# Two-layer attention and mixture-of-experts kernel: the second layer's chunked attention in a pipelined order, with transpositions and a second PSUM bank

## What is computed

```python
# attention of layer 1, 16 heads of 16, chunks of 128 tokens, S is the carried state of a head
scores  = einsum('bchd,bshd->bhcs', qb, kb) * D          # D: causal mask with a decay of each head
o_intra = einsum('bhcs,bshd->bchd', scores, vb)
o_inter = einsum('bchd,bhde->bche', qb, S) * q_decay
S_new   = chunk_decay * S + einsum('bshd,bshe->bhde', kb * k_decay, vb)
o = o_intra + o_inter                                     # then times sigmoid(gate)
o = o * rsqrt(mean(o*o over a head) + EPS) * norm_w       # group norm
attn = o @ Wo
# experts of layer 1: 8 experts, two for each token
y_e = (silu(x @ w_gate[e]) * (x @ w_up[e])) @ w_down[e]   # weighted and summed over the two experts
x = x + attn + moe
```

## Time and profile before

| | |
|---|---|
| median of 3 runs | 1006.86 us (1006.46 to 1008.85) |
| the profiled execution, its time | 1003.08 us |
| its span, first to last instruction | 1001.3 us |
| mean granted clock of PE, as a share of 2.4 GHz | 0.913 |
| busy: PE, DVE, ACT, POOL | 846.0, 574.8, 394.3, 312.0 us |

### The profile page before, as it was taken

One profiled execution on the slowest core, in us unless ns is written; L12 is line 12 of the kernel. 1 busy time (PEld: TensorE's weight loads), 2 busy tenths in 40 slices (PEclk: granted clock), 3 DMA queues, 4 the chain that ended last, 5 costly groups with the idle time before them and its releaser, 6 DMA issues. The chain is left out here.

```text
span 1001.3 us, 14864 instructions
## 1 busy us (share of the span) xinstructions
PE 846.0 (84%) x4544; PEld 486.2 (49%) x4544; DVE 574.8 (57%) x1269; ACT 394.3 (39%) x676; POOL 312.0 (31%) x250
## 2 busy tenths in 40 slices
PE   4989999858988997998988767399999899999963
PEld 3765655501223443433433546166666565666642
DVE  7746877268878776778673428234434333443437
ACT  2336666424664565466547413022222222222210
POOL 2034566363001331051015203233333443333231
PEclk9999999956998998999999966599999999999985
DMA  8524655462321332433403303899953444333243
GB/s 266 140 60 146 200 188 185 138 193 80 96 70 52 113 101 94 157 105 116 137 22 117 116 21 117 219 271 355 176 128 93 97 109 119 90 91 85 75 134 133
DMA packets 158354, 130.26 MB, mean 130 GB/s; under 512 B 64129, under 2 KB 139921, under 8 KB 158289
## 3 DMA queue, kind: packets, MB, share of 16 engines
q1 hardware_dynamic: 151136, 109.89, 38.0%
q0 software_dynamic: 7152, 19.54, 6.6%
HBM read 83.37 MB, written 46.01 MB: 129 GB/s over the span
## 5 line engine op out<-in xcount | busy, mean ns | idle before, releaser
L1305 DVE TENSOR_REDUCE b_negmax<-b_psM 128x1 f32<-128x512 f32 x256 | 163.0, 682 | 59.1 <-PE b_psM L1491 56.2
L1242 ACT ACTIVATE b_probs<-b_psE 128x512 f32<-128x512 f32 x256 | 138.8, 595 | 125.7 <-PE b_psE L1509 124.6
L1491 PE MATMUL b_psM<-b_kst,b_qst 96*128 96x512 bf16 x256 | 99.7, 432 | 38.5 <-DVE b_negmax L1305 22.5
L1509 PE MATMUL b_psE<-b_qst,b_kst 98*128 98x512 bf16 x256 | 88.1, 406 | 14.3 <-ACT b_probs L1242 9.6
L1863 POOL DMA_INDIRECT scratch_ys<-d_y,put x39 | 40.2, 1030 | 150.7 <-ACT d_y L1895 149.5
L2019 PE MATMUL d_psG<-d_w,d_xT 128*128 x156 | 76.6, 614 | 3.6 <-issue 1.7
L1518 PE MATMUL b_psV<-b_probs,b_vst 128*32 128x512 f32 x512 | 73.8, 650 | 3.1 <-ACT b_probs L1242 3.1
L2044 PE MATMUL d_psY<-d_w,d_hidden 128*128 x312 | 75.2, 384 | 0.0
L2027 PE MATMUL d_psU<-d_w,d_xT 128*128 x156 | 75.1, 604 | 0.0
L1491 PEld LDWEIGHTS b_psM<-b_kst,b_qst 96*128 96x128 bf16 x256 | 24.5, 99 | 98.4 <-DVE b_negmax L1305 73.5
L1509 PEld LDWEIGHTS b_psE<-b_qst,b_kst 98*128 98x128 bf16 x256 | 20.4, 99 | 103.2 <-issue 53.6
(11 more groups left out here) (353 smaller groups left out, 1593.6 us busy)
## 6 DMA issues: line engine op xcount, KB each, us to landing
scratch_parts<-a_parts SPq DMA_DIRECT2D x12, 512.0 KB, 4.3
b_qst<-scratch_parts SPq DMA_DIRECT2D x96, 64.0 KB, 2.1
b_kst<-scratch_parts SPq DMA_DIRECT2D x96, 64.0 KB, 2.1
scratch_parts<-b_part SPq DMA_DIRECT2D x24, 256.0 KB, 3.6
d_qst<-scratch_parts SPq DMA_DIRECT2D x96, 64.0 KB, 2.7
d_kst<-scratch_parts SPq DMA_DIRECT2D x96, 64.0 KB, 3.0
scratch_ys<-a_y SPq DMA_DIRECT2D x39, 128.0 KB, 1.8
scratch_v<-a_xn SPq DMA_DIRECT2D x4, 1024.0 KB, 6.9
```

The source lines that it names most:

```text
L1242: nc.scalar.activation(probs[k % PSLOTS][:, h, :], psE[h % 2][:, :], ACT.Exp, scale=float(HD) ** -0.5).then_inc(scores_used[h % 2], 1)
L1305: nc.vector.tensor_reduce(negmax[i][:, t, h:h + 1], psM[:, h % 2, :], AX_X, ALU.max, negate=True).then_inc(rows_used[h % 2], 1)
L1491: nc.tensor.matmul(psM[:, h % 2, :], qst[g][0:STACK, h, t * P:(t + 1) * P], kst[g][0:STACK, h, :], start=True, stop=True).then_inc(rows_re ...
L1509: nc.tensor.matmul(psE[h % 2][:, :], kst[g][0:STACKM, h, k * P:(k + 1) * P], qst[g][0:STACKM, h, :], start=True, stop=True).then_inc(score ...
```

## The change

- `main_order`: a chunk's steps are now `own` n, `outputs` n, `scores` 0 to 2 of chunk n+1, `normalise` n, `scores` 3 of chunk n+1, `turn_normed` n, `project` n. Nine steps a chunk instead of twelve, 148 in all instead of 192, with no empty ones, and all of them are dealt out over the expert rounds. Behind the last `down` come only `turn_normed` 15, `project` 15 and the four `combine`.
- `outputs` on PE turns `headsT` by four transpositions into ps0 in place of eight selection matmuls. The rows of a head then lie 32 columns apart (`spread`). The carried state's product goes into a bank of its own (psT, the first half of a new bank ps2).
- `gate_out` on DVE: for chunks with c > 0 it copies psT to `o`, adds `spread` to it, and then multiplies by `sg`, each behind the one before: three instructions ahead of `gated` instead of one. It now stands in the same step as `outputs`, as does POOL's power.
- Banks: `turn_normed` writes psT, `project` writes the other half of ps2 (psO).
- Waits: `scores` 0 of chunk n+1 waits for `gated` of chunk n instead of `o_done`; `scores` 1 for `update_done`; `outputs` and `project` for `o_done`; `turn_normed` for `normT_done`.
- SP no longer loads `sel` (32 KB). Its other loads, their order and their waits stay.

```diff
@@ main_order
-    steps = [(n, s) for n in range(CHUNKS) for s in range(LSTEPS)]
-    tail = LSTEPS + LSTEPS // 2
+    steps = [("scores", 0, g) for g in range(GROUPS)]
+    for n in range(CHUNKS):
+        ahead = [("scores", n + 1, g) if n + 1 < CHUNKS else ("rest", n, g) for g in range(GROUPS)]
+        steps += [("own", n, 0), ("outputs", n, 0), *ahead[0:3], ("normalise", n, 0), ahead[3],
+                  ("turn_normed", n, 0), ("project", n, 0)]
...
-            while given < (len(steps) - tail) * used // slots:
-                order.append(("light", *steps[given]))
+            while given < len(steps) * used // slots:
+                order.append(steps[given])
                 given += 1
-    combine = {4: 0, 6: 1, NORMALISE: 2, PROJECT: 3}
...
+    return order + [("combine", b, 0) for b in range(BATCHES)]
@@ layer1_main
-        ps0, ps1 = (ps(f"ps{i}", [P, SEQ]) for i in range(2))
+        ps0, ps1, ps2 = (ps(f"ps{i}", [P, SEQ]) for i in range(3))
+        spread = ps0[:, :].rearrange("p (h w) -> p h w", w=VW)
+        psT, psO = ps2[:, 0:KT * P], ps2[:, KT * P:KT * P + D]
@@ gate_out (DVE)
-                nc.vector.tensor_tensor(o[:, :], ps0[:, 0:D], sg[s][:, :], ALU.mult).then_inc(gated[s], 1)
+                mixed = o[:, :].rearrange("p (h d) -> p h d", d=HD)
+                if c:
+                    nc.vector.tensor_copy(o[:, :], psT).then_inc(carried, 1)
+                    dve.wait_ge(carried, 2 * (n - n // NC) - 1)
+                    nc.vector.tensor_tensor(mixed, spread[:, :, 0:HD], mixed, ALU.add).then_inc(carried, 1)
+                    dve.wait_ge(carried, 2 * (n - n // NC))
+                nc.vector.tensor_tensor(mixed, mixed if c else spread[:, :, 0:HD],
+                                        sg[s][:, :].rearrange("p (h d) -> p h d", d=HD), ALU.mult).then_inc(gated[s], 1)
@@ scores (PE)
-                    pe.wait_ge(o_done, n)
+                    if n:
+                        pe.wait_ge(gated[(n - 1) % CSLOTS], (n - 1) // CSLOTS + 1)
                 elif g == 1:
-                    pe.wait_ge(normT_done, n)
+                    pe.wait_ge(update_done, updates_before(n))
@@ outputs (PE)
+                updates(n)
...
+                pe.wait_ge(o_done, n)
+                for g in range(GROUPS):
+                    mm = nc.tensor.transpose(ps0[:, g * CH:(g + 1) * CH], headsT[:, g * CH:(g + 1) * CH], ident[:, :])
                 if c:
                     for k in range(KT):
-                        nc.tensor.matmul(ps0[:, k * P:(k + 1) * P], qd[n % CSLOTS][:, k * P:(k + 1) * P], state[:, k, :],
-                                         start=k == 0, stop=False, skip_group_check=True)
-                for g in range(GROUPS):
-                    mm = nc.tensor.matmul(ps0[:, g * HG * HD:(g + 1) * HG * HD], headsT[:, g * CH:(g + 1) * CH], sel[:, :],
-                                          start=c == 0 and g == 0, stop=g == GROUPS - 1, skip_group_check=True)
+                        mm = nc.tensor.matmul(psT[:, k * P:(k + 1) * P], qd[n % CSLOTS][:, k * P:(k + 1) * P],
+                                              state[:, k, :], start=True, stop=True, skip_group_check=True)
@@ turn_normed, project (PE)
-                    mm = nc.tensor.transpose(ps1[:, k * P:(k + 1) * P], normed[:, k * P:(k + 1) * P], ident[:, :])
+                    mm = nc.tensor.transpose(psT[:, k * P:(k + 1) * P], normed[:, k * P:(k + 1) * P], ident[:, :])
...
-                    mm = nc.tensor.matmul(ps0[:, 0:D], normT[:, k, :], wo[:, k, :], start=k == 0, stop=k == KT - 1)
+                    mm = nc.tensor.matmul(psO, normT[:, k, :], wo[:, k, :], start=k == 0, stop=k == KT - 1, skip_group_check=True)
```

More of the change, by code:

```diff
@@ L1673 @@
 UPDATES = NC - 1
-LSTEPS = 12
 CSLOTS = 3
-NORMALISE, TURN, PROJECT = LSTEPS - 3, LSTEPS - 2, LSTEPS - 1
 WCOLS = KT * H1 * 2 + HT1 * D
 def main_order():
-    steps = [(n, s) for n in range(CHUNKS) for s in range(LSTEPS)]
-    tail = LSTEPS + LSTEPS // 2
+    steps = [("scores", 0, g) for g in range(GROUPS)]
[3 more added lines that the diff above has]
+                  ("turn_normed", n, 0), ("project", n, 0)]
     order = [("turn", 0, 0), ("turn", 1, 0), ("gate", 0, 0), ("up", 0, 0), ("turn", 2, 0)]
@@ L1731, in layer1_main @@
         y = [sb(f"y{i}", [P, D]) for i in range(YSLOTS)]
-        ident, sel, blockmask = sb("ident", [P, P]), sb("sel", [P, HG * HD]), sb("blockmask", [P, P])
+        ident, blockmask = sb("ident", [P, P]), sb("blockmask", [P, P])
         normw, neghalf, wo = sb("normw", [P, D]), sb("neghalf", [P, HEADS]), sb("wo", [P, KT, D])
@@ L1755, in layer1_main @@
         heads_copied, update_ps, update_done, state_done = (sem(n) for n in ("heads_copied", "update_ps", "update", "state"))
+        carried = sem("carried")
         out_ps, squared, summed, ss_done, rs_done = (sem(n) for n in ("out_ps", "squared", "summed", "ss", "rs"))
@@ L1759, in layer1_main @@
         back_in, half_added, added, stored = sems("back_in", BATCHES), sem("half_added"), sem("added"), sem("stored")
-        CONSTS = 16 * 4
+        CONSTS = 16 * 3
         CHUNK_IN = 16 * (2 * len(Q_PARTS) + 4)
@@ L1818, in _ @@
             load_weights(1)
-            for dst, src in ((sel[:, :], io["sel16"]), (blockmask[:, :], io["blockmask"]),
+            for dst, src in ((blockmask[:, :], io["blockmask"]),
                              (normw[:, :], io["norm_w"].to_broadcast((P, D))),
@@ L1864, in down, with outputs @@
                                              y[b % YSLOTS][:, :], None).then_inc(put_out[b % YSLOTS], 16)
[L1866 to L1869, removed]
+            def outputs(n, _):
+                pool.wait_ge(ss_done, n + 1)
+                nc.gpsimd.tensor_tensor(rs[:, :], ss[:, :], neghalf[:, :], ALU.pow).then_inc(rs_done, 1)
             for b in range(XSLOTS):
@@ L1874, in _ @@
             pool.wait_ge(neghalf_set, 1)
-            walk({"light": light, "turn": turn, "down": down})
+            walk({"outputs": outputs, "turn": turn, "down": down})
         @block.scalar
@@ L1895, in down, with own, turn_normed @@
                 nc.scalar.activation(y[b % YSLOTS][:, :], psY[:, 0:D], ACT.Copy).then_inc(y_done, 1)
[L1897 to L1908, removed]
+            def own(n, _):
+                act.wait_ge(probs_used, n + 1)
+                act.wait_ge(out_ps, n)
+                nc.scalar.activation(headsT[:, :], ps0[:, :], ACT.Copy).then_inc(heads_copied, 1)
+            def turn_normed(n, _):
+                act.wait_ge(normT_ps, n + 1)
+                act.wait_ge(o_ps, n)
+                nc.scalar.activation(normT[:, :, :], psT.rearrange("p (k n) -> p k n", k=KT), ACT.Copy).then_inc(normT_done, 1)
+            walk({"own": own, "turn_normed": turn_normed, "gate": gate, "turn_h": turn_h, "down": down})
         @block.vector
@@ L1954, in gate_out, with normalise @@
                 nc.vector.tensor_scalar(ss[:, :], ss[:, :], 1.0 / HD, EPS, ALU.mult, ALU.add).then_inc(ss_done, 1)
-            def normalise(n):
+            def normalise(n, _):
                 dve.wait_ge(rs_done, n + 1)
@@ L1962, in normalise, with residual, outputs @@
                 nc.vector.tensor_tensor(normed[:, :], o[:, :], normw[:, :], ALU.mult).then_inc(normed_done, 1)
-            def residual(n):
+            def residual(n, _):
                 dve.wait_ge(o_ps, n + 1)
[L1966 to L1978, removed]
+                nc.vector.tensor_tensor(xacc[:, n, :], psO, xacc[:, n, :], ALU.add).then_inc(o_done, 1)
+            def outputs(n, _):
+                take_update(n)
+                gate_out(n)
             def combine(b, _):
@@ L1990, in combine @@
                     last.then_inc(added if i else half_added, 1)
-            walk({"light": light, "turn": turn, "up": up, "combine": combine})
+            walk({"scores": weigh, "outputs": outputs, "normalise": normalise, "project": residual, "turn": turn, "up": up,
+                  "combine": combine})
         @block.tensor
@@ L2060, in scores, with own @@
                 mm.then_inc(scores_ps[g], 1)
-            def own(n):
+            def own(n, _):
                 for g in range(GROUPS):
@@ L2079, in updates, with outputs @@
                 mm.then_inc(update_ps, 1)
-            def outputs(n):
+            def outputs(n, _):
                 c = n % NC
+                updates(n)
                 pe.wait_ge(consts_in, CONSTS)
@@ L2096, in outputs, with turn_normed @@
                 mm.then_inc(out_ps, 1)
-            def turn_normed(n):
+            def turn_normed(n, _):
                 pe.wait_ge(normed_done, n + 1)
-                if n % NC < NC - 1:
-                    pe.wait_ge(update_done, updates_before(n) + 1)
+                pe.wait_ge(normT_done, n)
                 for k in range(KT):
-                    mm = nc.tensor.transpose(ps1[:, k * P:(k + 1) * P], normed[:, k * P:(k + 1) * P], ident[:, :])
```

(9 more changed lines are left out.)

## The result

| | before | after |
|---|---|---|
| median, same session | 1006.66 us (14 runs) | 1000.75 us (14 runs) |
| ratio | | 0.9927 (0.9905 to 0.9948) |
| profiled execution: time, span | 1003.08, 1001.3 us | 995.34, 993.1 us |
| first `gate` of the last stage starts | 643.07 | 645.17 |
| last `down` starts | 961.03 | 965.62 |

A forecast was written before the change was run, and what follows sets the result against it. PE's work and waits were taken to bound the kernel until the last `down`, then a 38.4 us tail with DVE's `combine`. Terms -10.6 + 0.6 - 6.5 + 8.5 + 2.3 = -5.7 us gave 1001.2 us; range 990 to 1010.

The forecast's parts named there:

- The tail: After PE's end of the last `down`: 38.4 us replaced by bare combining of 27.8, -10.6 us, between -12 and -2.
- The rival with slow loads: In the tail: first `combine` only when all 4 MB are loaded back, +8 us, so 1009 us; chance 0.07.
- PE's work ahead of the last `down`: Transpositions save 0.40 us a chunk, -5.6 over 14 chunks; with the work added from chunks 14 and 15, together +0.6 us.
- (a): PE's wait in `turn_normed` for DVE's `normed` goes: at most 9.4 us, taken as 6.5.
- (b): `own` no longer follows `scores` 3 directly, so its wait for `probs` goes: 2.5 us saved.
- (c): The wait of scores for `o_done` is gone: -1.1 us.
- (d): The 2.07 us stall ending at 846 goes, and with it the half clock at 848 to 850: -1.7 us.
- (e): `scores` 0 of chunk n+1 now waits for `gated` n where short items cover it (n = 5, 7, 8, 10): +4.6 us.
- The rival in which it decides: DVE's chain to `gated` is longer, most covers fall short: for 1.0 us more, +4.8, 1011.7 us; chance 0.13.
- (f): `outputs` 11 has only `turn` ahead of it and waits 0.7 us for `headsT`.
- The late load: Ahead of chunk 3's `scores` 0 PE waits for its load: +8.5 us standing, +2.3 for half clock behind it.
- a rival in which they save nothing: In `outputs`: transpositions cost as much as the selection (+6.4 us) or run at half rate (+7.0), 1008 us; chance 0.10.

The follow-up runs named there:

- e2_before_early: The kernel before with chunk 3's loads issued between the weights of experts 5 and 6: 1.0011 of the kernel before (0.9994 to 1.0028), stage 358.4 us.
- e5_swap: The changed kernel with the banks of the score groups and their two waits swapped: 0.9805 of the kernel before (0.9772 to 0.9838), stage 340.6 us.
- e1_early: The changed kernel with chunk 3's sixteen loads issued between the weights of experts 5 and 6: 0.9845 of the kernel before, median 988.0 us.
- e10_split_combine: The changed kernel with swapped banks, early load and each batch's fourth combine tile on ScalarE and GpSimd: 0.9724 of the kernel before, median 980.2 us.

## Why the prediction was right, point by point

- **The tail** was forecast at -10.6 us and measured at -12.8. Its order of events is as forecast; the sizes were 2.1 us too long together. The scatter of block 37 did wait for the power, which ended at 966.5. But the last one, of block 38, waited only for ACT's copy of its rows (`[0.45 <-ACT d_y L1893]`) and started 0.9 us behind PE's end, as in the kernel before, and not 1.4: the power was over 0.9 us earlier than I had it. So SP resumed 3.4 us behind PE's end, not 4.0; the first pair of loads was in at 9.1, not 11 (from the first issue 5.7 us, where I had taken a landing of 6.5 and half a microsecond more); combining took 13.3, as said. The rival with slow loads falls: `combine` began at 976.46, before the last of the eight loads was issued (976.7).
- **PE's work ahead of the last `down`** can't be read by itself. The transpositions cost 0.44 us a chunk, as said, at full clock. The rule on transpose mode that I set against the edit (TensorE: Matmul & The Clock Gate of the Trainium skill, Part 4) does not show here: a group of four takes 0.44 us among matmuls at full clock.
- **Stalls that go.** (a) and (b) came as forecast: 9.4 to 0.3 and 2.2 to 0.4 us; (c), scores waiting for `o_done`, is gone. (d) failed: the half clock behind the stall at 846 did go, but one came behind a stall for `gated`, at 870 in the trace above and once in each of the other two of the changed kernel. Nor was the half clock a sure price of that stall: in e2_before_early the same stall of 2.07 us is there, and the `up` behind it runs at full clock (last section).
- **Stalls that come.** (e), the wait for `gated`: 3.9 us at four chunks, forecast 4.6 at four chunks. The rival in which it decides falls. But its price is not only its own: with the pauses ahead of gates and the clock, the edit that removes it (e5_swap) took 7.3 us off. (f), `outputs` 11 waiting for `headsT`, was 0.4 us where I had 0.7.
- **The late load.** Forecast 8.5 us of standing and 2.3 of half clock, measured 6.3 (708.55 to 714.86) and about 2.4 in the first trace, 5.5 to 6.9 of standing in the others. PE came to the wait when I had said, 63.4 us behind the first gate against 63.1. The load was earlier by 1.9: its last piece was issued 66.0 us behind the first gate, where I had 66.7 (67.3 before), and the wait ended 3.7 us later, not 4.9.
- Sum for the walk: forecast +4.9 (0.6 - 6.5 + 8.5 + 2.3), measured +2.5; without the late load's share -5.9 against -6.2. The stage: -5.7 forecast, -10.3 in the first trace, which the executions' own spread ahead of the stage (2.1 us in these two) partly hid in the spans. What was mis-sized is the tail and the load, by about 2 us each, both to the cautious side.
- So the mechanism was right and the near hit is in part luck. The forecast of -5.7 us lies by the difference of the first session's medians, -5.9, and within its interval; but the stage got shorter by 10.3 us and the other two chips say -11.2 (-13.7 to -8.5) and -10.1 (-12.5 to -7.8), nearly twice the forecast.
- A reading that was a little off: PE is not busy more than 18 of every 20 us in each stretch from 646 to 955. From 780 to 800 it is 17.65 and from 840 to 860 17.93, where the stalls of 1.5 and 2.1 us for `normed` lie. Nothing in the sum hangs on it.
- What the prediction took for granted and the experiments don't bear out is that the transpositions help: the order alone is as fast. It had a rival in which they save nothing because they cost PE as much as the selection. They cost PE half of it, and it is the longer chain behind them that takes the saving back.

## What to carry to other kernels

When an order is tightened so that all work is dealt out evenly, ask of each load when the new order first wants it and what stands ahead of it in the load queue: here one chunk came 15 us earlier than before, its load sat behind weights that no gate waited for even when they came later, and moving that load gave another 7.0 us on the chip on which the change gave 10.5. A short stall on the engine that bounds the kernel costs more than its length where the clock falls behind it; swapping two banks, so that the wait comes one step later, took 7.3 us off the stage, 6.2 without the 1.1 by which the stand for the late load happened to be shorter, where the waits' row says 3.9. And an operation that saves time on the bounding engine but lengthens a chain behind which that engine waits has to be measured in the order in which it will run: alone it gave 0.4%, inside the new order nothing that the times show.

## What the runs showed of the hardware

Stalls of 1.3 us for `gated`, followed by one short group and a pause of 0.6, were followed by a stretch of half clock on TensorE in five of eight cases: in the changed kernel's three traces at one of two such stalls each (868 to 873 in the first), in e1_early at both (803 to 808, 862 to 866). The stall of 1.1 us ahead of them was never followed by one. The same stall can go either way. In the kernel before the one of 2.07 us was followed by half clock; with the early load, in e2_before_early, it was not, and the next group began 1.72 us behind the `up`:

```profile
850.21 0.44 PE L2105 MATMUL d_ps<-d_ident,d_normed 128*128 128x128 f32 x2 [2.07 <-DVE d_normed L1964]
850.49 1.88 PE L2029 MATMUL d_psU<-d_w,d_xT 128*128 x4
852.21 1.03 PE L2112 MATMUL d_ps<-d_wo,d_normT 128*128 128x256 f32 x4
```

VectorE's `scalar_tensor_tensor` on 128x256 in SBUF took 0.48 us each, one starting every 0.40, with GpSimd idle. The eight that started while GpSimd added tiles of the same size took 0.83 to 0.95 us; beside ScalarE's activations alone they stayed at 0.48 (e10_split_combine).
